# Attention and feed-forward in one block, with the first tile's data prepared in attention's last group and a merged low-rank and gating product

## The reference

```python
q, k, v = x @ wq, x @ wk, x @ wv               # 32 query heads, 8 key heads of 32
scores = q @ k.T * SCALE, causal               # per head, 2048 x 2048
x = layernorm(x + (softmax(scores) @ v) @ wo)
h = relu(layernorm(x @ gw1.T + gb1) * ln_gamma + ln_beta)   # 32 wide
gates = h @ gw2.T + gb2                        # 8 experts
top_v, top_i = top_k(gates, 2); top_g = softmax(top_v)
w = weight of each expert per row, zero where an expert's count is over capacity (1536)
tmp = (x @ lora_A[e]) * w[e]                   # 8 experts of rank 16: 128 columns
out = layernorm(x + x @ weight.T + tmp @ lora_B / 16)
```

## Time and profile before

| | |
|---|---|
| median of 3 runs | 3563.53 us (3563.51 to 3566.39) |
| the profiled execution's own time | 3560.88 us |
| its span | 3559.1 us |
| PE busy | 3456.3 us, 97% |
| DVE, ACT, POOL busy | 56%, 41%, 46% |
| granted TensorE clock, mean | 0.988 |
| DMA share in the feed-forward's first stage | about 0.75 to 0.8 |

### The profile page before, as it was taken

One profiled execution on the slowest core, in us unless ns is written; L12 is line 12 of the kernel. 1 busy time (PEld: TensorE's weight loads), 2 busy tenths in 40 slices (PEclk: granted clock), 3 DMA queues, 4 the chain that ended last, 5 costly groups with the idle time before them and its releaser, 6 DMA issues. The chain is left out here.

```text
span 3559.1 us, 62842 instructions
## 1 busy us (share of the span) xinstructions
PE 3456.3 (97%) x25818; PEld 2440.5 (69%) x25818; DVE 1977.8 (56%) x3577; ACT 1468.6 (41%) x1839; POOL 1633.2 (46%) x702
## 2 busy tenths in 40 slices
PE   8999998999999999999999999999959999999999
PEld 7888885666666666666666666666538888888887
DVE  3121116777667677677767767777525666542222
ACT  3111112555555555555556555555542222221111
POOL 0000003877887798797788779879330000000000
PEclk9999997999999999999999999999989999999999
DMA  6344325021111111112111111110037877755553
GB/s 213 113 124 119 117 90 119 24 54 49 34 42 49 43 31 51 48 34 51 49 34 42 49 48 28 49 40 8 11 108 219 233 222 226 207 195 177 179 174 128
DMA packets 248223, 340.67 MB, mean 96 GB/s; under 512 B 55440, under 2 KB 150288, under 8 KB 247952
## 3 DMA queue, kind: packets, MB, share of 16 engines
q1 hardware_dynamic: 247952, 336.87, 32.1%
HBM read 203.08 MB, written 133.17 MB: 94 GB/s over the span
## 5 line engine op out<-in xcount | busy, mean ns | idle before, releaser
L684 DVE TENSOR_REDUCE p_part_max<-p_qm 128x1 f32<-128x512 f32 (+3 forms) x2240 | 1407.7, 671 | 597.4 <-PE p_qm L534 342.4
L504 POOL TENSOR_TENSOR p_psums<-p_psums,p_probs 128x1024 f32<-128x1024 f32 x575 | 1369.0, 2381 | 87.3 <-ACT p_probs L643 2.8
L647 ACT ACTIVATE p_probs<-p_km 128x1024 f32<-128x1024 f32 x896 | 879.8, 1022 | 480.7 <-PE p_km L562 404.5
L534 PE MATMUL p_qm<-p_k_st,p_q_st 96*128 96x512 f32 (+3 forms) x2560 | 912.8, 420 | 12.3 <-DMA p_q_st<-q_hi 10.8
L534 PEld LDWEIGHTS p_qm<-p_k_st,p_q_st 96*128 96x128 f32 x2560 | 480.9, 194 | 253.8 <-issue 112.6
L562 PE MATMUL p_km<-p_q_st,p_k_st 97*128 97x512 f32 x1792 | 599.6, 416 | 14.7 <-ACT p_probs L647 9.6
L569 PE MATMUL p_o<-p_probs,p_v 128*32 128x256 f32 (+1 forms) x9216 | 569.8, 371 | 0.0
L500 POOL TENSOR_TENSOR p_psums<-p_probs 128x1024 f32<-128x1024 f32 x110 | 262.2, 2384 | 353.8 <-ACT p_probs L647 353.8
L569 PEld LDWEIGHTS p_o<-p_probs,p_v 128*32 128x32 f32 x9216 | 270.6, 110 | 216.0 <-issue 44.2
L562 PEld LDWEIGHTS p_km<-p_q_st,p_k_st 97*128 97x128 f32 x1792 | 311.7, 191 | 114.3 <-ACT p_probs L647 70.9
L41 PE MATMUL p_acc<-p_xT_hi,p_w_hi 128*128 128x512 f32 x640 | 250.4, 391 | 9.7 <-DVE p_w_lo L226 9.7
(11 more groups left out here) (150 smaller groups left out, 4129.5 us busy)
## 6 DMA issues: line engine op xcount, KB each, us to landing
p_q_st<-q_hi SPq DMA_DIRECT2D x128, 256.0 KB, 4.7
p_x_raw<-in_xT SPq DMA_DIRECT2D x64, 256.0 KB, 3.5
q_hi<-p_out_hi SPq DMA_DIRECT2D x64, 256.0 KB, 2.0
q_lo<-p_out_lo SPq DMA_DIRECT2D x64, 256.0 KB, 2.3
p_q_st<-q_lo SPq DMA_DIRECT2D x64, 256.0 KB, 4.4
attended_T<-p_o_raw SPq DMA_DIRECT2D x128, 128.0 KB
p_a_raw<-attended_T SPq DMA_DIRECT2D x32, 512.0 KB, 5.2
p_recip<-reciprocals SPq DMA_DIRECT2D x128, 128.0 KB, 6.7
```

Of the source, the lines that this page charges most:

```text
L504: pool.tensor_tensor(sums[:, :, :], sums[:, :, :], probs[s % PB][:, :, :], ALU.add).then_inc(added, 1)
L534: last = pe.matmul(bank[:, x * keys:(x + 1) * keys], q_st[par][0:ROWS, c, h + x, sub * P:(sub + 1) * P], k_st[par][0:ROWS, j * CK:j * CK + ...
L647: act.activation(tile[:, :, :].rearrange("p h q -> p (h q)"), km[s % 2][:, :, :].rearrange("p a b -> p (a b)"), ACT.Exp, scale=SCALE).then ...
L684: dve.reduce_max(part_max[c][:, h:h + heads, sub, j], qm[bank_of(i)][:, 0:item_width(i)].rearrange("p (h k) -> p h k", h=heads), AX.X).the ...
```

## The change

- One block holds attention and feed-forward; each engine's feed-forward program follows its attention program. `over(engine)` waits for attention's last products, reads and stores. PE does not wait for it: it computes tile 0's product at once and waits for the PSUM banks' readers behind it.
- A new class `Opening` owns the output weight's tiles, tile 0's buffers and their work. In the last group SP loads the first batch's denominators behind step 34, the weight's pieces behind steps 36 to 50, stores reciprocals and loads tile 0 behind step 47; ACT converts the pieces behind steps 44, 46 to 58 and tile 0 behind step 62; DVE does its part after its last reduction. The second batch's denominators are loaded and inverted in feed-forward, and their reciprocals are stored in SP's step 1. Tiles of the last stage and group buffers share memory differently.
- The low-rank and gating product takes the high and low weights side by side: per k one matmul of 320 columns (high of the tile by both) and one of 160 (low of the tile by high), 16 instead of 24. ACT copies the second 160 columns out of PSUM, DVE adds them to the first in `hidden(t)` and gives low_done.

```diff
+    def send_reciprocals(self, sp):
+        sp.wait_ge(self.rec_done[0], 1)
+        for q in range(2):
+            sp.dma_start(self.rec_d[:, q * D:(q + 1) * D], self.den0[q * NH:(q + 1) * NH, :]
+                         ).then_inc(self.rec_stored[0], 16)
+        sp.dma_start(self.a_raw[:, :, :], self.aT_d[:, 0:P].rearrange("(k p) t -> p k t", p=P)).then_inc(self.a_in, 16)
+        sp.wait_ge(self.rec_stored[0], 32)
+        for h in range(REP):
+            sp.dma_start(self.recip0[h * HD:(h + 1) * HD, :, :],
+                         self.rec_d[h:NH:REP, 0:P].unsqueeze(0).to_broadcast([HD, KC, P])).then_inc(self.a_in, 16)
...
+    DEN_STEP, WO_STEP, SPLIT_STEP, REC_STEP = 34, 36, 44, 47
...
+                if last:
+                    events.append((DEN_STEP + 0.5, "denominators", 0))
+                    events.append((REC_STEP + 0.5, "reciprocals", 0))
+                    for k in range(KC):
+                        events.append((WO_STEP + 2 * k + 0.4, "load wo", k))
...
+                        if n == NG - 1:
+                            for k in range(KC):
+                                if s == SPLIT_STEP + 2 * k:
+                                    opening.split_wo(act, k)
+                            if s == SPLIT_STEP + 2 * KC + 2:
+                                opening.split_a(act)
...
+            over(sp)
             sp.wait_ge(a_lo_done, 1)
             load_a(1)
+            load_x(0)
             load_x(1)
...
                 for k in range(KC):
-                    last = matmul3(pe, ag_ps[:, 0:AG], yT_hi[:, k, :], yT_lo[:, k, :],
-                                   ag_hi[:, k, :], ag_lo[:, k, :], k == 0, k == KC - 1)
+                    pe.matmul(ag_ps[:, 0:2 * AG], yT_hi[:, k, :], ag_w[:, k, :], start=k == 0, stop=False)
+                    last = pe.matmul(ag_ps[:, 0:AG], yT_lo[:, k, :], ag_w[:, k, 0:AG], start=False, stop=k == KC - 1)
...
+            first_wo()
+            banks_read(pe)
             pe.wait_ge(ident_done, 2)
             pe.wait_ge(pool_const, 3)
-            first_wo()
...
-            def keep_low(t):
+            def copy_part(t):
                 act.wait_ge(ag_done, t + 1)
                 if t >= 2:
-                    act.wait_ge(low_stored[t % 2], 16 * (t // 2))
-                act.activation(low[t % 2][:, :], ag_ps[:, 0:ER], ACT.Copy).then_inc(low_done, 1)
+                    act.wait_ge(low_done, t - 1)
+                act.activation(part[t % 2][:, :], ag_ps[:, AG:2 * AG], ACT.Copy).then_inc(part_copied, 1)
...
             def hidden(t):
                 h = hid[t % 2]
                 dve.wait_ge(ag_done, t + 1)
+                dve.wait_ge(part_copied, t + 1)
+                if t >= 2:
+                    dve.wait_ge(low_stored[t % 2], 16 * (t // 2))
+                    dve.wait_ge(hidT_ps_done, t - 1)
+                dve.tensor_tensor(low[t % 2][:, :], ag_ps[:, 0:AG], part[t % 2][:, :], ALU.add).then_inc(low_done, 1)
                 dve.wait_ge(low_done, t + 1)
-                if t >= 2:
-                    dve.wait_ge(hidT_ps_done, t - 1)
-                dve.tensor_tensor(h[:, :], ag_ps[:, ER:AG], gb1_b, ALU.add).then_inc(h_done, 1)
+                dve.tensor_tensor(h[:, :], low[t % 2][:, ER:AG], gb1_b, ALU.add).then_inc(h_done, 1)
...
+            over(dve)
+            step(0)
             dve.wait_ge(pool_const, 3)
...
+            dve.wait_ge(den_in, 32)
+            dve.reciprocal(den1[2 * NH:4 * NH, :], den1[2 * NH:4 * NH, :]).then_inc(rec_done, 1)
             dve.wait_ge(small_in, 32)
             dve.wait_ge(experts_done, 1)
-            for t in range(NT + 3):
+            for t in range(1, NT + 3):
```

More of the change, by code:

```diff
@@ L2 @@
 from concourse import mybir
+from collections import namedtuple
 from contextlib import ExitStack
@@ L378, in attend, with over, banks_read, sync @@
         o_stored = [sem(f"p2_o_stored{i}") for i in range(2)]
-        block = ctx.enter_context(nc.Block())
-        @block.sync
-        def _(sp):
+        def over(engine):
+            engine.wait_ge(slot_done, NG * NSL)
+            engine.wait_ge(chunk_done, (NG - 1) * NCHUNK + LAST_SUMS.chunks[NC])
+            engine.wait_ge(o_read, NG * NC)
+            for i in range(2):
+                engine.wait_ge(o_stored[i], 16 * NG * NC)
+        def banks_read(pe):
+            pe.wait_ge(item_read, NG * NR)
+            pe.wait_ge(neg_done, NG * NK)
+            pe.wait_ge(o_read, NG * NC)
+        def sync(sp):
             def batch_head(n):
@@ L417, in store_o, with group @@
                              ).then_inc(o_stored[c % 2], 16)
-            def group(n, par, placed, load=True, more=True):
+            def group(n, par, placed, load=True, more=True, last=False):
                 b, g = batch_head(n)
@@ L472, in _, with gpsimd @@
             group(NG - 2, 0, STEADY, load=False)
-            group(NG - 1, 1, CLOSING, load=False, more=False)
+            group(NG - 1, 1, CLOSING, load=False, more=False, last=True)
             store_o(NG - 1, B - 1, NKV - 1, NC - 1)
[L475 to L479, removed]
+        def gpsimd(pool):
             make_identity(pool, ident, ident_done)
@@ L729, in feed_forward @@
     HALF = D // 2
-    EARLY = 2 * P
     ROWS = 3 * GH + E
@@ L852, in feed_forward, with gpsimd @@
         assert wm_step(KC - 1) < NT - 2
-        @block.gpsimd
-        def _(pool):
+        def gpsimd(pool):
+            over(pool)
             make_identity(pool, ident, ident_done)
@@ L930, in _ @@
                     load_a(t + 2)
+                if t == 1:
+                    sp.wait_ge(rec_done, 1)
+                    for q in range(2):
+                        sp.dma_start(rec_d[:, (2 + q) * D:(3 + q) * D], den1[(2 + q) * NH:(3 + q) * NH, :]
+                                     ).then_inc(rec_stored, 16)
+                    sp.wait_ge(rec_stored, 32)
                 for n in range(KC):
@@ L1415, in build, with _ @@
         project_qkv(nc, sem, xT, wq, wk, wv, q_hi, q_lo, k_hi, k_lo, v_d)
-        attend(nc, sem, q_hi, q_lo, k_hi, k_lo, v_d, aT_d, den_d)
-        feed_forward(nc, sem, x, aT_d, wo, wT, ag, lora_B, gw2T, rows, den_d, rec_d, y_d, yTh_d, yTl_d, low_d, out)
+        opening = Opening(nc, sem, ctx, wo, aT_d, den_d, rec_d)
+        attention, over, banks_read = attend(nc, sem, opening, q_hi, q_lo, k_hi, k_lo, v_d, aT_d, den_d)
+        mixing = feed_forward(nc, sem, opening, over, banks_read, x, aT_d, wT, ag, lora_B, gw2T, rows, den_d, rec_d,
+                              y_d, yTh_d, yTl_d, low_d, out)
+        block = ctx.enter_context(nc.Block())
+        @block.sync
+        def _(sp):
+            attention.sync(sp)
+            mixing.sync(sp)
+        @block.gpsimd
+        def _(pool):
+            attention.gpsimd(pool)
+            mixing.gpsimd(pool)
+        @block.tensor
+        def _(pe):
+            attention.tensor(pe)
+            mixing.tensor(pe)
+        @block.scalar
+        def _(act):
+            attention.scalar(act)
+            mixing.scalar(act)
+        @block.vector
+        def _(dve):
+            attention.vector(dve)
+            mixing.vector(dve)
 _INS = ["L0_attn_x", "L0_attn_wq", "L0_attn_wk", "L0_attn_wv", "L0_attn_wo", "L0_ffn_lora_B"]
```

211 lines of the change are left out of this document (117 added, 94 removed).

## The result

| | before | after |
|---|---|---|
| median | 3563.52 us (3562.76 to 3566.39, 4 runs) | 3618.23 us (3616.34 to 3620.52, 4 runs) |
| profiled execution, own time | 3560.88 | 3620.52 |
| its span | 3559.1 | 3618.7 |

The ratio is 1.0153, 95% interval 1.0137 to 1.0169: slower, as forecast, but by 54.7 us and not by 26.

The account below looks back on a forecast made before the run. PE, busy 97%, was taken to set the pace before. About 26 us won early, yet slower loop steps put tile 31 27.7 us later; less 1.8, +26 on 3563.5 gives about 3590 us, whole range 3532 to 3618.

Parts of the forecast that it names:

- The mechanism: Feed-forward loop: low store waits for the addition behind the division, so loads and stores alternate; 17.1 us per tile against 15.17.
- SP needs about 0.4 us for each issue: Loop, SP's queue: y store issued at 1.7 us after the low store, next load at 2.2.
- the closing stage, which the diff leaves alone: Last stage, after the feed-forward loop: assumed untouched by the change, with no term of its own in the sum.
- the start: Hand-over to tile 5's second half: earlier first tiles win about 26 us.
- attention: Attention's last group: nine inserted ACT activations delay its end by 3.2 us, bounds 0 and 9.5.
- the sign: Whole kernel: slower, by 26 us; chance of slower 0.68, same 0.05, faster 0.27.
- the merged product: Low-rank and gating product: 2.07 us per tile against 2.68, 0.6 less, lost in the loop while PE idles.
- the line: Merged product: line through measured 256- and 512-column starts, giving 0.147 us for a 320-column product.
- 6.8 + 8.6 + 1.7: Loop per tile: stores until y ends 6.8, load landing 8.6, divide, addition and hand-overs 1.7; sum 17.1 us.
- before each tile's first product: Loop: PE idle 2 to 3 us there, released by p_a_lo or p_hid.
- the three forecast: Attention's last group: exposed splits after steps 48, 52 and 56, 1.06 us each, 3.2 us in all.
- the three merged products at -1.8: Behind tile 31 in PE's order: three remaining merged products save 1.8 us.

Follow-up runs that it names:

- e1: Changed kernel with VectorE's addition that gives low moved ahead of the division of the next row tile: 3538.83 us, ratio 0.9931.
- e2: Changed kernel with only SyncE's low store moved from the head of its step to behind the row tile's load: 3536.95 us, ratio 0.9927.
- e3: Changed kernel with the earlier 24 products of 160 columns in place of the merged product, single block and opening kept: 3557.51 us, ratio 0.9984.
- e9: Changed kernel with addition ahead of division, weight splits behind steps 41, 46, 51, 59, 32-byte-offset padding, second reciprocal, its stores and feed-forward weight later: 3525.46 us.
- e11: e1 plus only padding that puts a_hi0, a_lo0, p4_yT_hi and p4_yT_lo 32 bytes past a multiple of 128: 3543.7 us, ratio 0.9943.
- e10: e9 with SyncE's low store also moved behind the load of the row tile: 3523.82 us, ratio 0.9892.
- e13: e10 with other padding, placing stationary tiles a multiple of 256 bytes from the matrices they are multiplied with: 3514.91 us, ratio 0.9863.
- e6: e1 plus 32 bytes of padding ahead of the closing stage's transposed tiles p4_yT_hi and p4_yT_lo: 3539.5 us, ratio 0.9937.
- e12: Kernel before with 96 bytes of padding ahead of its a_hi and a_lo tiles and 32 behind them: 3573.21 us, ratio 1.003.
- e14: Changed kernel with only the padding of e13: 3609.19 us, ratio 1.0129.

## Why the prediction was right or wrong

The mechanism was forecast, its price was not: 59.6 us between the spans for 26. The largest miss is one term of the loop's sum: the time from one low store to the next load, 2.2 us by "SP needs about 0.4 us for each issue", was 3.16, and the loop 17.64 us for 17.1, 14.0 us over 26 tiles. The rest are 7.9 us in "the closing stage, which the diff leaves alone", 7.3 at the start and 4.4 in attention, each below. All four went the same way.

**Right: the mechanism and the sign.** The low store goes out directly behind the addition, and that behind the division; the division waits 5.2 to 7.6 us for p_recip (the prediction had 7 and more); the DMA engines are at zero from 2713 to 2715 and their share is under 0.75; e1 and e2 take the coupling away at either end and the loss with it.

**Right: the merged product.** Pairs start 0.258 us apart (six from 2733.22 to 2734.77; the line gave 0.147 + 0.112), 2.06 us for 2.07. By the Trainium skill, "TensorE: Matmul & The Clock Gate", section "Back-to-back issue gap", 16 isolated products would be 1.64 us. The same section adds that its formula counts too little at small N, which the prediction leaves out and the trace bears out (2.06 for 1.64). e1's loop shows the saving (14.47 and 14.71 against e3's 15.10 and 15.33, which has the same buffers in place).

**Wrong size: the loop, 17.64 for 17.1, +14.0 us.** Of my sum "6.8 + 8.6 + 1.7" two parts held: load issued to divided 13.06 us on average (19 tiles; 13.2 meant), divided to low store 1.49 (1.7). The part that failed is "SP needs about 0.4 us for each issue": the issue of the y store kept SP for 1.3 us (before 0.67 on average), in the microseconds in which the DMA engines filled (share 0.70 at 2716 and 1.01 at 2719, in the last fence), so the load went out 3.16 us behind the low store and not 2.2. The rows had a warning: 0.67 in the earlier trace rows and 1.44 in the earlier trace rows.

**Wrong place: where PE waits.** I had it idle "before each tile's first product". It stands before the merged product (0.5 to 3.1 us, released by p_low) and in most tiles 1.06 us before the transpose of the hidden rows. I had named only SP's queue behind low_done and not PE's own wait on it. The pace was not changed by that, as e2 shows.

**Wrong: the start, -18.3 for -25.6.** PE's stop ahead of tile 1, which answers to the 7.23 us of the earlier trace rows, was 5.31 us (5.4 forecast):

```profile
2649.22 0.77 PE L42 MATMUL p_acc<-p_wo_hi,p_a_hi 128*128 128x512 f32 x1 [5.31 <-DVE p_a_lo L1306]
```

Then DVE:

```profile
2654.21 6.55 DVE L1436 RECIPROCAL p_den<-p_den 64x1024 f32<-64x1024 f32 x1
2660.79 1.23 DVE L1328 TENSOR_TENSOR p_y<-p_acc,p_x 128x1024 f32<-128x1024 f32 x1
...
2678.34 1.23 DVE L1302 TENSOR_TENSOR p_a_raw<-p_a_raw,p_recip 128x1024 f32<-128x1024 f32 x1 [6.50 <-DMA p_recip<-reciprocals]
```

The length was right (6.5), the place was not. The prediction puts it right behind the split of tile 1; it began 5.1 us after that (2649.1), since the splitting of the gating weight stands ahead of it and waits for a load that was issued behind tile 1's. Its stores, behind tile 3's load, then held SP until 2678.97, so that five transfers went out directly ahead of tile 4's load, which took 13.4 us from issue (2681.94) to division. e9, which moves both the reciprocal and its stores, gains 9.5 us there against e11.

**Wrong: attention, +7.65 for +3.2.** The exposed splits were the three forecast: 1.13, 0.90 and 1.13 us. PE and the clock at the first of them:

```profile
2586.11 1.22 PE L669 MATMUL p_km<-p_q_st,p_k_st 97*128 97x512 f32 x2 [1.13 <-ACT p_probs L753]
```

```profile
2585.00:2586.00 1.00, 0.00 (x0) 0.00 (x0) 0.82 (x1) 1.00 (x3) 0.86 (x2) 0.89 0.58 124
2586.00:2587.00 1.00, 0.89 (x2) 0.50 (x2) 0.40 (x1) 1.00 (x3) 1.00 (x1) 0.50 0.78 184
...
2591.00:2592.00 1.00, 1.00 (x9) 0.31 (x2) 0.00 (x0) 0.00 (x0) 0.93 (x1) 0.50 0.33 62
2596.00:2597.00 1.00, 1.00 (x6) 0.26 (x8) 0.00 (x0) 1.00 (x2) 0.00 (x0) 0.51 0.67 269
2607.00:2608.00 1.00, 1.00 (x16) 0.58 (x12) 0.64 (x1) 1.00 (x2) 1.00 (x1) 0.50 0.00 0
```

The step that failed is a term that the sum left out, the clock. It was at the low level, 1.2 GHz, in three stretches of 6.8, 3.4 and 3.4 us; before has one such stretch there (3.4 us from 2586), and so has e9, without exposed splits; e1, with them, has two. The three stops make 3.2 us of the 7.65. An estimate from these rows: the 10.2 us more at half the clock can make up to 5.1, which covers the other 4.5. That the stops bring the further ones is likely and not shown, since e10 and e13 have two without such stops. The stretches vary between executions, and with them attention's end (2629.05 to 2633.60 in the kernels with three exposed splits).

**Wrong: the end, +6.1 for -1.8.** "The closing stage, which the diff leaves alone" is the step that failed. The new block moved its buffers: 28 tiles x (12.64 - 12.46) = 5.0 us (that padding alone changes this pace, e6, e12 and e14 show). PE also stood 2.02 us before the first main product (3194.16), where it had not stood before. The load of that product's tile landed at 3194.07; it stands in SP's queue behind a low store that went out at 3183.86, right behind DVE's addition (3183.51). So this stop, too, seems to come from where low_done is given; e1 has none there. With the three merged products at -1.8 that is 5.2 of the 6.1 us.

## What to carry to other kernels

When a completion signal moves from one engine to another, list what each in-order queue has behind its wait: here a 0.3 us addition, placed behind the wait for a load, held back all that stood behind it in SP's queue, the next load too, and cost 79 us; moving the addition up one place, or moving the store that waits for it behind the load, took all of that back. Splits slipped into another stage are free only in slots where the trace shows a pause, and when their data has landed. A stage that a diff does not touch can still change pace when its buffers move; compare its time per tile first.

## What the runs showed of the hardware

**Where buffers lie.** The same products, with no wait between them, took 12.37 to 12.53 or 12.64 to 12.73 us per tile by the distance between stationary tile and moving matrix modulo 256 bytes (table above). In most of a slow tile the 54 products start 0.231, 0.231 and 0.238 us apart in turn, in a fast one 0.226, 0.229 and 0.232.

**The clock.** After a stop of 2.10 us (PE resumes at 2714.78) the granted clock fell to the low level 0.7 us later, in a stretch in which PE was busy throughout:

```profile
2714.00:2715.00 1.00, 0.21 (x1) 0.22 (x2) 0.93 (x4) 0.47 (x1) 0.00 (x0) 1.00 0.00 0
2715.00:2716.00 1.00, 1.00 (x7) 1.00 (x7) 0.74 (x3) 0.77 (x2) 0.00 (x0) 0.75 0.22 66
2716.00:2717.00 1.00, 1.00 (x5) 1.00 (x5) 0.96 (x3) 0.00 (x0) 0.00 (x0) 0.50 0.70 90
...
2719.00:2720.00 1.00, 1.00 (x6) 0.82 (x5) 0.96 (x3) 0.00 (x0) 0.00 (x0) 1.00 1.01 414
```

The same followed the stops of 3.13 us (2820.86) and 2.38 us (2857.97), and also those of 1.79 (2997.92) and 1.89 us (3069.15), but not those of 2.09 (2839.51) and 2.52 us (3173.73): in these rows the length of the stop alone does not decide. In the loop it probably cost little, since the loop waited for transfers; no run separates this.
